# Seven block additions and a constant moved from GpSimd to VectorE, and routing and scaling pieces moved between chunks

## What is computed

```python
h = _ln_c(x)                                       # layer norm over the 64 channels of a pixel
a = conv3x3(sign(h + move1), sign(w3) * mean|w3|)
a = rprelu(h + bn(a))                              # rprelu: add, leaky slope, add, per channel
b = conv1x1(sign(a + move2), sign(w_pw) * mean|w_pw|)
b = rprelu(bn(b) + a)
x = x + b                                          # "the block"
t = tokens(x)                                      # 32 * 3136 tokens of 64 channels
u = _ln_t(t)
e = argmax(softmax(u @ gate_w + gate_b))           # one of 8 experts
y = relu(u @ w1[e] + b1[e]) @ w2[e] + b2[e]        # only within the expert's capacity
t = t + nan_to_num(y * prob * kept)
```

## Time and profile before

| | us |
|---|---|
| median of 3 runs | 1737.37 (1737.23 to 1741.01) |
| the profiled execution | 1731.63 |
| its span in the trace | 1729.8 |
| TensorE busy | 1544.1 (89%) |
| VectorE busy | 1438.9 (83%) |
| ScalarE busy | 1232.6 (71%) |
| GpSimd busy | 1051.5 (61%) |
| granted clock of TensorE, mean | 0.942 of full speed |

### The profile page before, as it was taken

How to read it: one execution, slowest core, us unless ns; L and a number is a source line. 1 busy time by engine, 2 the same in 40 slices (tenths; PEclk the granted TensorE clock), 3 DMA queues, 4 the chain that set the end, 5 groups by cost and what they waited for, 6 DMA issues and landing times.

```text
span 1729.8 us, 40181 instructions
## 1 busy us (share of the span) xinstructions
PE 1544.1 (89%) x10344; PEld 836.6 (48%) x10344; DVE 1438.9 (83%) x3653; ACT 1232.6 (71%) x4066; POOL 1051.5 (61%) x1054
## 2 busy tenths in 40 slices
PE   7998988888888988888762899999999999999996
PEld 2343444344433444334432555556666666666664
DVE  4588888979888898888987587888888888888887
ACT  4788777878788777787662676777777767777762
POOL 3115557656766668666676775666566666665664
PEclk9999998999999999998875899999999999999997
DMA  9446767765667366543355676888999999999998
GB/s 253 84 111 135 176 141 177 173 156 130 173 137 183 118 106 169 151 115 97 92 129 146 178 204 179 238 243 281 308 292 306 290 307 295 335 314 316 305 301 293
DMA packets 304112, 351.80 MB, mean 203 GB/s; under 512 B 48804, under 2 KB 254596, under 8 KB 298084
## 3 DMA queue, kind: packets, MB, share of 16 engines
q1 hardware_dynamic: 260516, 261.02, 55.6%
q0 software_dynamic: 41120, 85.81, 15.9%
q10 hardware_dynamic: 2336, 3.54, 0.6%
HBM read 179.70 MB, written 180.01 MB: 208 GB/s over the span
## 4 chain that ended last, share of the span: by engine, by line
PE 55%; issue 13%; DVE 10%; POOL 9%; ACT 5%; SPq 4%; DMA 2%; POOLq 0%; ACTq 0%; DVEq 0%
PE bank L885 12%; PE bank L895 11%; PE bank L876 7%; POOL pairs_by_group L516 5%; PE bank L786 4%; PE bank L903 4%; PE bank L748 3%; POOL X L510 3%; PE bank L845 3%; PE bank L917 2%; PE bank L796 2%; PE bank L819 2%; SPq L635 2%; SPq L627 1%; ACT SQR L1022 1%
## 5 line engine op out<-in xcount | busy, mean ns | idle before, releaser
L516 POOL DMA_INDIRECT pairs_by_group<-ROWS,idx x400 | 433.9, 1085 | 119.5 <-issue 113.6
L548 POOL DMA_INDIRECT results_by_pair<-X,PAIRNO x310 | 308.6, 996 | 179.8 <-issue 99.7
L1042 ACT ACTIVATE X<-bank,X 128x256 f32<-128x256 f32 x693 | 283.4, 471 | 49.5 <-PE bank L885 49.1
L510 POOL TENSOR_TENSOR X<-Z,X 128x448 f32 (+1 forms) x112 | 143.3, 1280 | 251.5 <-DVE Z L1381 232.7
L885 PE MATMUL bank<-X 64*128 64x256 f32 x1848 | 263.9, 404 | 0.0
L895 PE MATMUL bank<-X 128*64 128x256 f32 x1848 | 250.5, 392 | 0.8 <-DVE X L1408 0.8
L786 PE MATMUL bank<-S,WB 128*128 128x448 bf16 x1008 | 227.1, 373 | 0.0
L1035 ACT ACTIVATE X<-bank 128x256 f32<-128x256 f32 x231 | 88.5, 383 | 167.5 <-PE bank L876 167.0
L548 POOL DMA_INDIRECT results_by_pair<-S,PAIRNO x152 | 149.7, 985 | 94.2 <-PE bank L876 65.3
L885 PEld LDWEIGHTS bank<-X 64*128 64x128 f32 x1848 | 159.9, 187 | 50.5 <-issue 39.7
L876 PE MATMUL bank<-ident,X 128*64 128x128 f32 x1848 | 153.3, 287 | 22.2 <-DMA X<-pairs_by_group 17.5
(11 more groups left out here) (231 smaller groups left out, 3001.1 us busy)
## 6 DMA issues: line engine op xcount, KB each, us to landing
X<-weights_by_group SPq DMA_DIRECT2D x231, 258.5 KB
X<-pairs_by_group SPq DMA_DIRECT2D x231, 134.0 KB
pairs_by_group<-PAD SPq DMA_DIRECT2D x15, 1742.0 KB, 20.1
X<-in_x_dram SPq DMA_DIRECT2D x16, 1568.0 KB, 7.9
block_output<-X SPq DMA_DIRECT2D x112, 224.0 KB, 2.6
ROWS<-block_output SPq DMA_DIRECT2D x16, 1568.0 KB
Z<-results_by_pair SPq DMA_DIRECT2D x15, 1568.0 KB
out_dram<-ROWS SPq DMA_DIRECT2D x14, 1568.0 KB
```

The lines of the kernel that those rows point to most:

```text
L510: pool.tensor_tensor(X2[:, j * CW:(j + 1) * CW], Z[:, p.z(j * CW)], X[:, p.x(j * CW, CW)], ALU.add).then_inc(s_x2, 1)
L516: pool.indirect_dma_start(rows, bass.IndirectOffsetOnAxis(ap=idx[0:m, p.odd, k:k + 1], axis=0), ROWS[0:m, p.odd, k, :], None).then_inc(s_s ...
L548: pool.indirect_dma_start(done, bass.IndirectOffsetOnAxis(ap=PAIRNO[:, u, j:j + 1], axis=0), RES[u][:, j, :], None,).then_inc(s_back[u], 16)
L1042: last = A(HB[:, ring % 2, q, :], hidden(q), ACT.Relu, bias=WR[:, ring, at:at + 1])
```

## The change

The block addition with the constant goes to VectorE: `add_block` becomes one scalar_tensor_tensor, Z + CB + X, right after the second slope of the same chunk, with the same three waits. GpSimd keeps the scatters alone. Since X2 now holds CB, the bias row goes with its tile, its semaphore, its matmul, VectorE's set-up and L815; row products start their bank themselves. L1438 loses its constant. Routing pieces 15 and 16 move from chunk 0 to chunk 1. The scaling slices 0 to 4, which stood in chunks 3, 4, 4, 4 and 5, stand in chunks 2, 2, 4, 5 and 6. The diff, cut:

```diff
-            def add_block(p, j):
-                wait_apart(pool, s_q2, p.n * NCH + j + 1)
-                wait_apart(pool, s_x2s[j], p.n * 16)
...
-                wait(pool, s_tr, (p.n - 1) * NG + old + 1)
-                pool.tensor_tensor(X2[:, j * CW:(j + 1) * CW], Z[:, p.z(j * CW)], X[:, p.x(j * CW, CW)],
-                                   ALU.add).then_inc(s_x2, 1)
...
-            def bias_row():
-                pe.wait_ge(s_gw, 1)
-                mm(PRE[0:KROWS, 0:GW], col(CB).to_broadcast([P, KROWS]), row_weights[:, :],
-                   start=True, stop=True).then_inc(s_setp, 1)
...
-                                pe.wait_ge(s_br, 1)
-                            m = len(group_tiles[g])
-                            mm(ROWP[g][:, 0:m * GW], ones[0:KROWS, :], biasrow[:, 0:m, :].rearrange("p k w -> p (k w)"),
-                               start=True, stop=False)
+                                pe.wait_ge(s_gw, 1)
                             for k in group_tiles[g]:
                                 at = k % RGROUP * GW
                                 last = mm(ROWP[g][:, at:at + GW], X2[:, k * P:(k + 1) * P],
-                                          row_weights[:, :], start=False, stop=k == group_tiles[g][-1])
+                                          row_weights[:, :], start=True, stop=True)
...
+            def add_block(p, j):
+                wait_apart(dve, s_q2, p.n * NCH + j + 1)
+                wait_apart(dve, s_x2s[j], p.n * 16)
...
+                wait(dve, s_tr, (p.n - 1) * NG + old + 1)
+                V.scalar_tensor_tensor(out=X2[:, j * CW:(j + 1) * CW], in0=Z[:, p.z(j * CW)], scalar=col(CB),
+                                                       in1=X[:, p.x(j * CW, CW)], op0=ALU.add, op1=ALU.add).then_inc(s_x2, 1)
...
-                    if rou and c == 5:
-                        scale_rows(rou, 4)
+                    if rou and c >= 5:
+                        scale_rows(rou, c - 2)
...
-                    if old and c == 0:
+                    if old and c == 1:
                         route(old, 15)
...
-                    if rou and c == 4:
-                        scale_rows(rou, 1)
                     if late:
...
+                        add_block(late, j)
-                    if old and c == 0:
+                    if old and c == 1:
                         route(old, 16)
...
-                    if rou and c in (3, 4):
-                        scale_rows(rou, 0 if c == 3 else 2)
+                    if rou and c == 2:
+                        scale_rows(rou, 0)
+                        scale_rows(rou, 1)
                     if rou and c == 4:
-                        scale_rows(rou, 3)
+                        scale_rows(rou, 2)
...
-                V.scalar_tensor_tensor(out=part, in0=image_bank(odd, g)[:, 0:GROUP * PP],
-                                       scalar=col(CB), in1=part, op0=ALU.add, op1=ALU.add).then_inc(s_c3, 1)
+                V.tensor_tensor(part, image_bank(odd, g)[:, 0:GROUP * PP], part, ALU.add).then_inc(s_c3, 1)
```

More of the change, by code:

```diff
@@ L203, in metaformer_kernel @@
         cst = sb("cst", [P, 32])
-        biasrow = sb("biasrow", [KROWS, RGROUP, GW], bf16)
         RT = part_of(X, P, RING, SUB, 2 * UNIT)
@@ L269, in metaformer_kernel @@
         s_gw = sem("gate_weights_ready")
-        s_br = sem("bias_row_ready")
         s_x2 = sem("block_ready")
@@ L501, in _ @@
                     pool.wait_ge(s_bb, k + 3)
-            def add_block(p, j):
-                wait_apart(pool, s_q2, p.n * NCH + j + 1)
-                wait_apart(pool, s_x2s[j], p.n * 16)
-                old = next(g for g in range(NG) if last_chunk[g] >= j and (g + 1) * RGROUP * P >= (j + 1) * CW
-                           or g == NG - 1)
-                wait(pool, s_tr, (p.n - 1) * NG + old + 1)
-                pool.tensor_tensor(X2[:, j * CW:(j + 1) * CW], Z[:, p.z(j * CW)], X[:, p.x(j * CW, CW)],
-                                   ALU.add).then_inc(s_x2, 1)
             def scatter_tiles(p, first, end):
@@ L518, in scatter_tiles, with one_pass @@
                         ROWS[0:m, p.odd, k, :], None).then_inc(s_sc[p.odd][k // RGROUP], 16)
-            def one_pass(con, rou, sca):
+            def one_pass(sca):
                 for c in range(NCH):
-                    late, j = (con, c - 1) if c else (rou, NCH - 1)
                     if sca and c:
@@ L528, in one_pass @@
                         scatter_tiles(sca, (c - 1) * TILES // (NCH - 1), c * TILES // (NCH - 1))
-                    if late:
-                        add_block(late, j)
             def run(i, odd):
                 pick = lambda k: Pair(i + k, (odd + k) % 2) if not isinstance(i, int) or 0 <= i + k < PAIRS else None
-                one_pass(pick(0), pick(-1), pick(-2))
+                one_pass(pick(-2))
             for i in range(4):
@@ L753, in center_chunk @@
                     sign_weights()
-                if alone and c == NCH - 1:
-                    bias_row()
             def group_piece(p, q):
@@ L1300, in write_order @@
                 V.tensor_scalar(order[:, :], bank[1][0:1, SUPER:SUPER + EARLY], -1.0, None, ALU.add).then_inc(s_order, 1)
+            def add_block(p, j):
+                wait_apart(dve, s_q2, p.n * NCH + j + 1)
+                wait_apart(dve, s_x2s[j], p.n * 16)
+                old = next(g for g in range(NG) if last_chunk[g] >= j and (g + 1) * RGROUP * P >= (j + 1) * CW
+                           or g == NG - 1)
+                wait(dve, s_tr, (p.n - 1) * NG + old + 1)
+                V.scalar_tensor_tensor(out=X2[:, j * CW:(j + 1) * CW], in0=Z[:, p.z(j * CW)], scalar=col(CB),
+                                                       in1=X[:, p.x(j * CW, CW)], op0=ALU.add, op1=ALU.add).then_inc(s_x2, 1)
             def scale_rows(p, i):
@@ L1308, in scale_rows @@
                                 ALU.mult).then_inc(s_sl, 1)
[L1310 to L1324, removed]
             def one_pass(cen, nor, con, rou, old):
@@ L1386, in one_pass @@
                             mark_full()
-                    if norm and not con and c == 2:
-                        bias_rows()
                     if rou and c >= 2:
                         route(rou, {2: 1, 3: 4, 4: 7, 5: 10, 6: 13}[c])
-                    if rou and c in (3, 4):
-                        scale_rows(rou, 0 if c == 3 else 2)
+                    if rou and c == 2:
+                        scale_rows(rou, 0)
+                        scale_rows(rou, 1)
                     if rou and c == 4:
-                        scale_rows(rou, 3)
+                        scale_rows(rou, 2)
             software_pipeline(dve, one_pass)
```

## The result

The changed kernel takes 1808.3 us (median of four runs, 1806.5 to 1811.1) against 1739.2 for the kernel before: a ratio of 1.040, 95% interval 1.037 to 1.042. Slower was forecast, but by 1.1%, and 1808 lies above the range of 1721 to 1786. The profiled execution took 1806.5 us, with a span of 1804.2.

A forecast was written before the change was run, and what follows sets the result against it. VectorE, with the ScalarE and TensorE steps it waits for in turn, was taken to set the pass; 11 passes at +1.6 us, 3 at +1.3, less 2 at the start, made +19.5 us: 1757 us, +1.1%, range 1721 to 1786.

The follow-up runs named there:

- a_idx0_unroll: The changed kernel with routing pieces 15 and 16 back in chunk 0 and VectorE's loop written out: 1716.0 us, ratio 0.987.
- a_idx0_unroll2: The changed kernel with routing pieces 15 and 16 back in chunk 0 and the loop written out on VectorE and ScalarE: 1704.9 us, ratio 0.982.

## What to carry to other kernels

Before moving work off a chunk, list who waits for its last result, and follow each waiter's whole queue: here 2.6 us of index arithmetic, moved by one chunk, held ScalarE by 7 us through a buffer that GpSimd's scatters had to free, and TensorE with it. Scatters landed 2.4 us after their issue (median) with neither clear nor table beside them and 5.9 with both, so price a release through DMA by a row's time from issue to landing under the same traffic, and add it to the new time of issue. When a loop body grows, look at its branch: here 0.3 us became 2.8 to 3.1 on VectorE.

## What the runs showed of the hardware

A scatter issued while the 1742 KB clear ran moved no packet for 4.0 us, and the read that waits for the third one followed its issue by 8.8 us (median of passes 3 to 13); without the clear and the tables the first packet came after 1.5 us and a scatter landed after 2.4.

The stop at the branch of VectorE's loop took 0.3 us in the kernel before, 2.8 to 3.1 in the changed one and 7.7 to 8.0 with the clear in flight. ScalarE's loop stops as well: written out, the index rows of the passes behind its branch no longer come 1.1 to 3.6 us late (a_idx0_unroll against a_idx0_unroll2).

Waits on counts held in registers, standing as instructions of their own, were not free on VectorE: two of them ahead of an addition left it idle for 0.50 us, the same waits on constants for 0.04.
